# Fronts of two groups side by side: the front's steps move to earlier slots and its self projections to another PSUM bank

## The chip, the cores and the metric
One core of a Trainium2 chip runs the whole program. The metric is device time in microseconds (us) of one execution, the median of several runs. TensorE (PE) does matrix products into the eight banks of PSUM, VectorE (DVE) and ScalarE (ACT) do elementwise work and read PSUM, GpSimd (POOL) does elementwise work in SBUF and issues scattering DMAs, and SyncE (SP) issues the other DMAs. Each engine works through its own queue in order; semaphores couple them.

## The reference
The input is x of 64 batches by 64 tokens by 128 features, a context of the same shape and a mask. Three stages follow one another:

```
h  = layernorm(x)                                   # per token
q, k, v = LN(h Wq), LN(ctx Wk), LN(ctx Wv)          # 16 heads of 8; LN with gamma, beta
q', k' = relu(q) + eps, (relu(k) + eps) * mask;  v = v * mask
att = (q' (k'^T v)) / (q' sum(k') + eps)            # linear attention, per head
x1 = x + LN(att Wd + bd)
z  = layernorm(x1);  h = LN1(z)
x2 = z + softmax(causal(q k^T / sqrt 8)) v Wp + bp  # q, k, v from h: causal self attention
a  = LN2(x2); logits = a Wg + bg; two best of 8 experts, weights by softmax
out = x1 + x2 + sum over the two experts of  w_e (gelu(a W1_e + b1_e) W2_e + b2_e)
```

Mean removal of q, k, v and of the dense output is folded into the weights, so only sums of squares are left of those norms.

## The kernel before
The 4096 tokens are taken as 8 groups of 512 (four tiles of 128 tokens, two batches a tile). Each group passes through a *front* (linear attention up to the self attention's q, k, v), eight *units* of self attention (a tile and half of the heads each), a *back* (output projection, norm, gate logits, two best experts, slots) and a scatter of its rows to DRAM, sorted by expert. When all groups are done, an expert loop of 71 blocks of 128 rows runs, and the results are gathered.

`schedule` (L263) writes the order out by hand, the same for all four compute engines. Each has a function `slot(n, unit, nxt, later, prev, routed)` and a *beat* calls it for n = 0 to 7. In beat k, slot n does unit n of group k, and beside it pieces of the front of group k+1 (`nxt`), of the first norm and the transposes of group k+2 (`later`), of the back of group k-1 (`prev`), and of the routing of group k-2 (`routed`). Ahead of the beats stand `opening(0)`, `front(0)` and `opening(1)` in a line. Beats 2 to 5 are a loop of two turns with two beats each; the others are written out. `finish` does the back of group 7.

A unit on PE: `subtract_max(n)` (waits for the row maxima that DVE took of the scores, `score_max`), `scores(n+1)` (waits for the keys `km`, which POOL multiplies out in `head_keys`), `probs_values(n-1)`, `probs_T(n)`. ACT takes exp in between and copies the transposed probabilities. So PE runs at most one unit ahead of DVE's maxima.

PSUM banks: two for scores, one for transposed probabilities, one for probabilities times values, three front banks F0, F1, F2, and `end_bank` for the transposes of x and context and for the back. Front of group k+1 in beat k before the change, by slot:

- 0: PE `project_k`, `project_q`, `project_v` into F1, F2, F0; ACT `squares`; POOL `x_and_mask`
- 1: DVE `qkv_sums` (one sum over all three); POOL `qkv_scale` (one power)
- 2: DVE `qkv_normal`, `keys_affine`; POOL `values`
- 3: PE `q_T`, `key_sums`, `key_values`; DVE `q_eps`, `key_values`
- 4: PE `linear_attention` in two parts; DVE `divide`
- 5: PE `attention_T`, `dense`; ACT `copy_aT`, `square_o`; DVE `o_sums`; POOL `o_scale`
- 6: DVE `residual` (x1 and its moments); POOL `zh_scale`
- 7: DVE `h_normal`; PE `h_T`, `project_self` into F1, F2, F0; ACT `copy_hT`, `keys`; DVE `unit0_keys`, `queries`; then in slot 0 of the next beat DVE `self_values`, `z_normal`

`later` has `x_moments`, `x_scale` in slot 5 and `x_normal`, `context_T`, `x_T` in 7. `prev` has `y_T` in 0, `project_out` on PE in 1 and on DVE in 3, `a_scale` and `keep_residual` on POOL in 3, `a_normal` in 4, `a_T` in 5, `gate_logits` and `copy_logits` in 6, `top_two` and `gates` in 7. `routed` has `ranks` and `slots` in 2 and two of eight scatters in each of slots 4 to 7.

Of the kernel before, what the change touches and what calls it, by code (L numbers as in the profile page):

```python
# [22 lines left out]
def xattn_attention_moe(nc: bass.Bass, a, out):  # L23
# [28 lines left out]
    with ExitStack() as ctx:  # L52
# [6 lines left out]
        def sems(names):  # L59
# [56 lines left out]
        xa = place[5][:, 2, :, :]  # L116

# [11 lines left out]
        rs = sb("rs", [P, 3 * T])  # L129
        ss = sb("ss", [P, 3 * T])  # L130
        kvz = sb("kvz", [P, T, BPT, HD + 1, 32])
# [67 lines left out]
         kf_ps, qf_ps, vf_ps, km0_ok, km_ok, s_ps, mx_ok, sm_ps, p_ok, pT_ps, pT_ok, y_ok, pv_ps, yT_ps, yT_ok,  # L199
         f_ps, a_ok, aT2_ps, h2T_ok, lg_ps, consts, w_ready, res_ok, mid_ps, y2_ps, sq_ok, o2_ok, dl_ok, e_ok, mid_ok, setup, x_var, x_rstd, x1_ok,  # L200
         ss_ok, qkv_rstd, value_step, oss_ok, o_rstd, z_var, z_rstd, z_ok, zb_ok, a_var, a_rstd, xa_ok, xs_b,
         sum_ok, kn_ok, key_step, den_step, osum_ok, og_ok, zs_b, kb0_ok, rden_ok, as_b, top_ok, topi_ok, gate_step, zeroed, centred,
# [4 lines left out]
            "kv_ps kvz_ok qp_ok au_ps att_ok aT_ps aT_ok o_ps h_ok hT_ps hT_ok kf_ps qf_ps vf_ps km0_ok km_ok "  # L207
# [3 lines left out]
            "z_ok zb_ok a_var a_rstd xa_ok xs_b sum_ok kn_ok key_step den_step osum_ok og_ok zs_b kb0_ok "  # L211
# [51 lines left out]
        def schedule(eng, opening, front, slot, finish):  # L263


            def beat(k, u):
                fixed = isinstance(k, int)
                nxt = None if fixed and k + 1 >= GROUPS else (k + 1, 1 - u)
                later = None if fixed and k + 2 >= GROUPS else (k + 2, u)
                prev = None if fixed and k < 1 else (k - 1, 1 - u)  # L270
                routed = None if fixed and k < 2 else (k - 2, u)
                for n in range(UNITS):
                    slot(n, (k, u), nxt, later, prev, routed)
# [21 lines left out]
        with nc.Block() as block:  # L295
# [79 lines left out]
            def _(pe):  # L375
# [13 lines left out]
                def context_T(k, u):  # L389
                    pe.wait_ge(c_loaded[u], (k // 2 + 1) * 16)  # L390
                    if isinstance(k, int) and k == 1:
                        pe.wait_ge(xT_ok, 1)
                    elif not (isinstance(k, int) and k < 3):
                        pe.wait_ge(lg_ok, k - 2)
# [8 lines left out]
                def project_k(k):  # L403
                    pe.wait_ge(cT_ok, k + 1)
                    if not (isinstance(k, int) and k == 0):
                        pe.wait_ge(kf_ok, k)
                    per_tile(F1, cT, wx[:, 1, :]).then_inc(k_ps, 1)

                def project_q(k):
                    pe.wait_ge(xT_ok, k + 1)  # L410
                    if not (isinstance(k, int) and k == 0):
                        pe.wait_ge(qbd_ok, 2 * k)
                    per_tile(F2, xnT, wx[:, 0, :]).then_inc(q_ps, 1)

                def project_v(k):
                    if not (isinstance(k, int) and k == 0):
                        pe.wait_ge(vbd_ok, k)
# [14 lines left out]
                def key_values(k):  # L432
                    pe.wait_ge(vp_ok, k + 1)
                    pe.wait_ge(qr_ok, k + 1)
                    for b in range(BPT):
                        for t in range(T):
# [3 lines left out]

                def linear_attention(k, part):


# [3 lines left out]
                    for c in range(HD + 1):  # L447
                        dst, at = (front_bank[part], c * S) if c < HD else (F2, part * S)
                        for b4 in range(4):
                            t, b = 2 * part + b4 // 2, b4 % 2  # L450
                            last = pe.matmul(dst[b4 * 32:b4 * 32 + 32, at:at + S], kvz[:, t, b, c, :],  # L451
                                             qp[:, t * P + b * S:t * P + b * S + S], start=True, stop=True)
                    last.then_inc(au_ps, 1)

                def attention_T(k):
                    pe.wait_ge(att_ok, k + 1)
                    for part in range(2):
                        for n4 in range(4):
                            last = pe.transpose((F2, F0)[part][:, n4 * P:n4 * P + P],
                                                att[:, part, n4 * P:n4 * P + P], ident[:, :])  # L460
                    last.then_inc(aT_ps, 1)

                def dense(k):
                    pe.wait_ge(aT_ok, k + 1)
                    pe.matmul(t4(F1[:, :]), ones_r[:, :], over_t(db_hi[:, :]), start=True, stop=True)
                    pe.matmul(t4(F1[:, :]), ones_r[:, :], over_t(db_lo[:, :]), start=False, stop=True,
                              skip_group_check=True)
                    for t in range(T):
                        last = pe.matmul(t4(F1[:, :])[:, t, :], xnT[:, t * P:t * P + P], wx[:, 3, :],
# [7 lines left out]
                def project_self(k):  # L477
                    pe.wait_ge(hT_ok, k + 1)
                    h = h1T[:, :, :].rearrange("p t n -> p (t n)")
                    pe.matmul(F1[:, :], wf[:, 1, :], h, start=True, stop=True).then_inc(kf_ps, 1)  # L480
                    pe.matmul(F2[:, :], wf[:, 0, :], h, start=True, stop=True).then_inc(qf_ps, 1)  # L481
                    per_tile(F0, h, wf[:, 2, :]).then_inc(vf_ps, 1)


                def scores(k, u, n):
                    if n == 0:
                        pe.wait_ge(qbd_ok, 2 * k + 1)
                        pe.wait_ge(km0_ok, k + 1)
                    else:
                        if n == 1:  # L490
                            pe.wait_ge(qbd_ok, 2 * k + 2)
                        pe.wait_ge(km_ok, k * (UNITS - 1) + n)
# [34 lines left out]
                def y_T(k, u):  # L527
                    pe.wait_ge(y_ok, (k + 1) * T)

                    opened = k + 3  # L530
                    pe.wait_ge(xT_ok, min(opened, GROUPS) if isinstance(k, int) else opened)
                    if not (isinstance(k, int) and k == 0):
# [7 lines left out]
                def a_T(k, u):  # L540
                    pe.wait_ge(a_ok, k + 1)
                    transposes(end_bank, send[u][:, :, 0, 0:D]).then_inc(aT2_ps, 1)

                def gate_logits(k):
                    pe.wait_ge(h2T_ok, k + 1)
                    lg = end_bank[:, 0:T * E].rearrange("p (t e) -> p t e", t=T)
# [19 lines left out]
                def opening(k, u):  # L566
                    context_T(k, u)
                    x_T(k)

                def front(k, u):  # L570
# [946 lines left out]
```

## Time and profile before

| | us |
|---|---|
| median of 3 runs | 775.77 (774.07 to 776.71) |
| the profiled execution | 775.02, span 773.2 |
| PE busy | 579.9 (75%) |
| DVE busy | 426.1 (55%) |
| POOL busy | 321.8 (42%) |
| ACT busy | 230.8 (30%) |
| mean granted TensorE clock | 0.822 of full |

Busy time is time in which an engine executes an instruction; the span is from the first instruction to the last. PE work shows longer where the clock was granted at half, so its busy time is no fixed amount of work.

### The profile page before, as it was taken

To read this page: it belongs to the slowest core of one execution; us is meant where nothing else is said; L and a number is where in the kernel's file an instruction comes from. 1 tells how busy PE (TensorE), PEld (TensorE's weight loads), DVE (VectorE), ACT (ScalarE), POOL (GpSimd) and SP (SyncE) were. 2 spreads that over 40 slices of the span, in tenths; PEclk is the share of its full clock that TensorE was granted. 3 is DMA by queue.
4 is the path that set the end of the run, shared out by engine and by line. 5 is a ranking of instruction groups with operands and counts; after the bars stand their busy time and mean duration, and the time that the engine had idled before them with its cause. 6 is when DMAs were issued, how large, how long until landed. Compare 5 with 4: busy or idle time off the path is not lost.

```text
span 773.2 us, 15557 instructions
## 1 busy us (share of the span) xinstructions
PE 579.9 (75%) x4384; PEld 461.9 (60%) x4385; DVE 426.1 (55%) x1285; ACT 230.8 (30%) x559; POOL 321.8 (42%) x327
## 2 busy tenths in 40 slices
PE   0463897988877978978879778795249999998960
PEld 0362576666655657656566566564148887787860
DVE  4424456686767676576685774673513433333435
ACT  0101313414313403313322331331024444444430
POOL 5302341451464563463562562463714334334340
PEclk9755758887979878879787898797559999999995
DMA  5996260250430250170000000000135555555639
GB/s 131 176 205 108 62 78 2 68 71 1 92 54 15 77 76 8 31 120 14 14 0 7 22 0 9 14 8 28 41 106 158 149 158 153 157 158 147 166 95 322
DMA packets 90461, 63.85 MB, mean 83 GB/s; under 512 B 16302, under 2 KB 77105, under 8 KB 90420
## 3 DMA queue, kind: packets, MB, share of 16 engines
q1 hardware_dynamic: 86100, 54.86, 33.0%
q0 software_dynamic: 4320, 8.47, 3.1%
q8 instruction: 22, 0.36, 0.2%
q14 instruction: 19, 0.16, 0.1%
HBM read 35.18 MB, written 28.58 MB: 82 GB/s over the span
## 4 chain that ended last, share of the span: by engine, by line
PE 55%; DVE 15%; issue 11%; ACT 4%; SPq 4%; POOL 4%; DMA 3%; DVEq 1%; another core or an unknown queue 1%; ACTq 0%; POOLq 0%
PE bank L678 9%; PE bank L667 7%; PE bank L497 6%; PE bank L522 5%; PE bank L380 4%; PE bank L451 4%; PE bank L437 3%; PE bank L385 2%; PE bank L480 2%; DVE places L1102 2%; PE bank L509 2%; PE bank L429 2%; PE bank L481 2%; POOL sorted_rows L983 2%; PE bank L502 2%
## 5 line engine op out<-in xcount | busy, mean ns | idle before, releaser
L1046 POOL DMA_INDIRECT result_rows<-back,rows x71 | 69.4, 978 | 117.6 <-DVE back L1466 109.8
L845 ACT ACTIVATE mid<-bank,b 128x128 f32<-128x128 f32 x284 | 81.2, 369 | 92.3 <-PE bank L667 80.5
L522 PEld LDWEIGHTS bank<-vbd,pT 128*128 128x128 f32 x512 | 74.6, 216 | 44.4 <-issue 24.2
L963 POOL TENSOR_TENSOR km<-kb,head 128x512 f32<-128x512 f32 x56 | 59.5, 1069 | 80.2 <-ACT kb L752 49.1
L678 PE MATMUL bank<-w,mid 128*128 x568 | 83.8, 292 | 11.0 <-ACT mid L845 9.2
L678 PEld LDWEIGHTS bank<-w,mid 128*128 128x128 f32 x568 | 71.2, 194 | 24.2 <-issue 23.0
L667 PE MATMUL bank<-hT,w 128*128 128x128 f32 x568 | 83.0, 291 | 3.1 <-DMA w<-in_L_ffn_exp_W_dram 1.6
L522 PE MATMUL bank<-vbd,pT 128*128 128x36 f32 x512 | 74.2, 295 | 13.9 <-ACT pT L765 13.1
L914 POOL TENSOR_TENSOR rs<-ve,minus_half 128x12 f32<-128x12 f32 (+2 forms) x24 | 39.8, 1660 | 97.4 <-DVE ve L1149 48.5
L667 PEld LDWEIGHTS bank<-hT,w 128*128 128x128 f32 x568 | 71.1, 197 | 5.9 <-issue 4.4
L497 PE MATMUL bank<-km,qbd 128*128 128x512 f32 x128 | 73.3, 658 | 0.0
L765 ACT COPY pT<-bank 128x512 f32<-128x512 f32 x64 | 37.8, 590 | 117.7 <-PE bank L509 110.3
L1213 DVE TENSOR_REDUCE mx<-bank 128x8 fp32r<-128x512 f32 x64 | 44.1, 689 | 48.4 <-PE bank L497 48.0
L983 POOL DMA_INDIRECT sorted_rows<-send,slot_u x64 | 63.4, 990 | 16.7 <-issue 16.7
L385 PE MATMUL bank<-ident,places 128*128 128x128 f32 x160 | 33.8, 352 | 45.3 <-DVE places L1069 23.1
L759 ACT ACTIVATE pr<-bank 128x512 f32<-128x512 f32 x64 | 38.6, 602 | 93.0 <-PE bank L502 85.5
L1461 DVE TENSOR_TENSOR plain<-bank,b 128x128 f32<-128x128 f32 x71 | 20.7, 291 | 66.2 <-PE bank L678 35.9
L1455 DVE TENSOR_SCALAR hT<-bank,cols 128x128 f32<-128x128 f32 x71 | 29.1, 410 | 50.0 <-PE bank L659 49.5
L385 PEld LDWEIGHTS bank<-ident,places 128*128 128x128 f32 x160 | 25.3, 190 | 51.7 <-DVE places L1069 25.8
L509 PE MATMUL bank<-ident,pr 128*128 128x128 f32 x256 | 42.1, 289 | 0.2 <-issue 0.2
L502 PE MATMUL bank<-mx,neg_ident 128*128 128x512 f32 x64 | 32.6, 509 | 6.6 <-DVE mx L1213 6.5
L429 PE MATMUL bank<-emb,places 128*128 128x2 f32 x64 | 14.6, 350 | 27.1 <-DVE places L1111 27.1
(187 smaller groups left out, 1004.1 us busy)
## 6 DMA issues: line engine op xcount, KB each, us to landing
w<-in_L_ffn_exp_W_dram SPq DMA_DIRECT2D x79, 256.0 KB, 3.4
sorted_rows<-blank SPq DMA_DIRECT2D x64, 260.0 KB, 7.6
rows<-sorted_rows SPq DMA_DIRECT2D x71, 65.0 KB
places<-result_rows SPq DMA_DIRECT2D x16, 256.0 KB, 5.5
places<-in_ctx_dram SPq DMA_DIRECT2D x8, 256.0 KB, 2.9
places<-in_x_dram SPq DMA_DIRECT2D x8, 256.0 KB, 3.8
out_dram<-acc SPq DMA_DIRECT2D x8, 256.0 KB, 5.9
result_rows<-back,rows POOLq DMA_INDIRECT x71
```

What stands on the lines that cost most here:

```text
L385: last = pe.transpose(t4(psum[:, :])[:, t, :], src[:, t, :], ident[:, :])
L497: pe.matmul(bank_n[:, :], qbd[u][:, n % 2, n // 2, :], km[n % 2][:, :, :], start=False, stop=True).then_inc(s_ps, 1)
L502: pe.matmul(score_bank[n % 2][:, :], neg_ident[:, :], mx[:, n % 2, :].unsqueeze(2).broadcast_to([P, HG, S]), start=False, stop=True, skip_ ...
L509: last = pe.transpose(probT_bank[:, j * P:j * P + P], pr[:, n % 2, j * P:j * P + P], ident[:, :])
L522: last = pe.matmul(pv_bank[:, hp * W:hp * W + W].rearrange("p (b c) -> p b c", b=BPT), pT[:, j, :], vbd[u][:, t, :, hp, :], start=True, st ...
L667: last = pe.matmul(hidden[2 * (s % 2) + c // 2][:, c % 2 * P:c % 2 * P + P], w1[s % 4][:, c * P:c * P + P], hT[s % 2][:, :], start=True, s ...
L678: last = pe.matmul(result[s % 2][:, 0:D], mid[s % 2][:, c, :], w2[:, bass.ds(expert, 1), c, :].rearrange("p o d -> p (o d)"), start=c == 0 ...
L845: A(mid[s][:, c, :], hidden[2 * s + c // 2][:, c % 2 * P:c % 2 * P + P], ACT.Gelu, bias=b1[:, bass.ds(expert, 1), c]).then_inc(mid_ok, 1)
L963: G.tensor_tensor(km[n % 2][:, :, :], kb[u][:, n % 2, t * S:t * S + S].unsqueeze(1).broadcast_to([P, HG, S]), head8[:, :].unsqueeze(2).bro ...
L983: G.indirect_dma_start(out=sorted_dram, out_offset=bass.IndirectOffsetOnAxis(ap=slot_u[u][:, j // 2, t:t + 1], axis=0), in_=send[u][:, t, ...
L1046: G.indirect_dma_start(out=result_dram, out_offset=bass.IndirectOffsetOnAxis(ap=rows[s][:, D:D + 1].bitcast(U32), axis=0), in_=back[s % 4] ...
L1213: V.tensor_reduce(mx[:, n % 2, :], score_bank[n % 2][:, :].rearrange("p (h k) -> p h k", h=HG), AX.X, ALU.max).then_inc(mx_ok, 1)
```

## The change
What it does, part by part:

- `schedule` has no `opening` and `front` any more. The beats start at k = -2: beats -2 and -1 have no unit, only pieces of the groups 0 and 1.
- The front of a group is spread over two beats. As `later` (group k+2): `x_moments` in slot 1, `x_normal` in 2, `context_T` and `x_T` in 3, `project_k` and `project_q` in 5, `project_v` and the sums in 6, `qkv_normal` and `values` in 7. As `nxt` (group k+1): `q_T`, `key_sums`, `key_values` in 0, `linear_attention` and `divide` in 1, `attention_T`, `dense`, `o_sums` in 2, `residual`, `o_scale`, `zh_scale` in 3, `h_normal` and `h_T` in 4, self keys and queries, `z_normal` in 5, self values in 6.
- `project_self` is split: keys and values go to `end_bank`, one after the other, queries to F0. The waits on the banks follow (`gate_logits`, `a_T`, `y_T`, `context_T`, `project_k`, `project_v`).
- `prev`: DVE's `project_out` and POOL's `a_scale`, `keep_residual` in slot 2, `a_normal` in 3, `a_T` in 4, `gate_logits` and `copy_logits` in 7. `routed`: `ranks` and `slots` in 4, scatters 2, 2 and 4 in slots 5, 6 and 7.
- Squares, sums and powers are done for each of k, q, v by itself. Keys are scaled by their norm and gamma in one instruction per tile; values are scaled by norm times mask, and beta times mask is a new tile `vb`, so POOL's `values` has two steps for three. The attended transpose has a tile `aT` of its own, the norms of the dense output and of x1 have small tiles of their own.
- The denominators of the linear attention are computed first and signalled by themselves (`den_ps`); `divide`, `attention_T` and `copy_aT` go by halves.
- `unit0_keys` leaves DVE: POOL's `head_keys` does all eight, two slots ahead of their unit.

The core of the diff (declarations, and edits that say the same again, are left out):

```diff
-            opening(0, 0)
-            front(0, 0)
-            opening(1, 1)
-            beat(0, 0)
-            beat(1, 1)
+            for k in range(-2, 2):
+                beat(k, k % 2)
...
 PE, slot
                     if prev:
                         if n == 0:
                             y_T(*prev)
                         if n == 1:
                             project_out(prev[0])
-                        if n == 6:
+                        if n == 4:
+                            a_T(*prev)
+                        if n == 7:
                             gate_logits(prev[0])
                     if nxt:
+                        if n == 0:
+                            q_T(nxt[0])
+                        if n == 1:
+                            linear_attention(nxt[0], 0)
+                        if n == 2:
+                            attention_T(nxt[0])
+                        if n == 6:
+                            self_values(nxt[0])
+                    if later:
+                        if n == 3:
+                            context_T(*later)
+                        if n == 5:
+                            project_k(later[0])
+                            project_q(later[0])
+                    if unit:
+                        probs_T(k, n)
+                    if nxt:
                         if n == 0:
                             key_sums(nxt[0])
                             key_values(nxt[0])
+                        if n == 1:
+                            linear_attention(nxt[0], 1)
+                        if n == 2:
+                            dense(nxt[0])
+                        if n == 4:
+                            h_T(nxt[0])
+                        if n == 5:
+                            self_keys(nxt[0])
+                            self_queries(nxt[0])
+                    if later:
+                        if n == 3:
+                            x_T(later[0])
+                        if n == 6:
+                            project_v(later[0])
...
 DVE, slot (new order; score_max(n+1), slots in 4 and attended stand first)
+                    if nxt:
+                        if n == 0:
+                            q_eps(nxt[0])
+                            key_values(nxt[0])
+                        if n == 1:
+                            divide(nxt[0])
+                        if n == 2:
+                            o_sums(nxt[0])
+                        if n == 3:
+                            residual(*nxt)
+                        if n == 4:
+                            h_normal(*nxt)
+                        if n == 5:
+                            z_normal(*nxt)
+                            queries(*nxt)
+                    if later:
+                        if n == 1:
+                            x_moments(*later)
+                        if n == 2:
+                            x_normal(*later)
+                        if n == 5:
+                            mask_columns(*later)
+                        if n == 6:
+                            sums(later[0], 0)
+                            sums(later[0], 1)
+                    if prev:
+                        if n == 2:
+                            project_out(*prev)
+                        if n == 3:
+                            a_normal(*prev)
+                    if nxt and n == 6:
+                        self_values(*nxt)
+                    if later:
+                        if n == 6:
+                            sums(later[0], 2)
+                        if n == 7:
+                            qkv_normal(later[0])
...
 POOL, slot
+                    if unit and n + 2 < UNITS:
+                        head_keys(*unit, n + 2)
+                    if unit and n == 0:
+                        z_bias(*unit)
+                    if prev and n == 2:
                         a_scale(prev[0])
                         keep_residual(*prev)
+                    if nxt:
+                        if n == 3:
+                            o_scale(nxt[0])
+                            zh_scale(nxt[0])
+                        if n == 6:
+                            head_keys(*nxt, 0)
+                        if n == 7:
+                            head_keys(*nxt, 1)
+                    if routed and n == 5:
+                        scatter_waits(*routed)
+                    if later:
+                        if n == 1:
+                            x_scale(later[0])
+                        if n == 5:
+                            x_and_mask(*later)
+                        if n == 6:
+                            qkv_scale(later[0])
+                        if n == 7:
+                            values(later[0])
+                    if routed and n >= 5:
+                        for j in ((0,), (1,), (2, 3))[n - 5]:
+                            scatter(*routed, j)
```

## Rows read from the trace of the kernel before

**Rows 1.** The page: busy time of PE, and the granted clock in 40 slices.
```profile
PE 579.9 (75%) x4384; PEld 461.9 (60%) x4385; DVE 426.1 (55%) x1285; ACT 230.8 (30%) x559; POOL 321.8 (42%) x327
PEclk9755758887979878879787898797559999999995
```
**Rows 2.** Windows cut at beats' first exps: length, busy by engine, PE clock, DMA share, GB/s.
```profile
83.69:142.30 58.61, 51.65 (x367) 39.20 (x367) 34.29 (x84) 16.44 (x30) 20.35 (x17) 0.73 0.30 47
...
258.21:319.91 61.70, 51.53 (x398) 39.45 (x398) 41.41 (x129) 18.32 (x34) 30.58 (x27) 0.81 0.27 53
...
443.11:503.80 60.69, 48.77 (x390) 36.49 (x390) 39.08 (x116) 17.23 (x32) 30.12 (x28) 0.83 0.03 10
503.80:526.83 23.03, 21.96 (x139) 16.06 (x138) 16.20 (x59) 9.37 (x18) 14.38 (x14) 1.00 0.05 16
...
526.83:566.90 40.07, 10.59 (x56) 8.84 (x55) 14.58 (x74) 3.37 (x8) 20.62 (x21) 0.56 0.10 33
```
**Rows 3.** Chain that ended last, beat from 258.21: start, us, what.
```profile
274.59 1.64 DVE places L1109
276.26 1.16 DVE places L1111
277.46 1.87 PE bank L429 x8
279.33 3.02 PE bank L437 x16
```
**Rows 4.** Windows of two beats with the granted clock, columns as in rows 2.
```profile
256.00:276.00 20.00, 15.78 (x104) 11.54 (x102) 14.96 (x32) 7.16 (x13) 13.01 (x12) 1.00 0.63 121
276.00:286.00 10.00, 8.54 (x34) 6.88 (x34) 7.11 (x18) 0.60 (x1) 6.36 (x6) 0.50 0.27 38
288.00:303.00 15.00, 12.92 (x168) 9.89 (x162) 8.31 (x27) 4.77 (x9) 4.52 (x5) 1.00 0.05 16
...
250.00:254.00 4.00, 3.49 (x4) 1.52 (x5) 0.56 (x4) 1.79 (x4) 0.00 (x0) 0.50 0.05 17
```
**Rows 5.** Timeline, PE: start, us, line, out<-in, count, idle before.
```profile
250.51 2.08 PE L480 MATMUL bank<-h1T,wf 128*128 128x512 f32 x2 [0.87 <-ACT h1T L746]
...
259.54 1.95 PE L380 MATMUL bank<-wx,places 128*128 128x128 f32 x16
...
262.58 0.46 PE L502 MATMUL bank<-mx,neg_ident 128*128 128x512 f32 x1
...
266.11 0.46 PE L502 MATMUL bank<-mx,neg_ident 128*128 128x512 f32 x1
...
277.46 1.87 PE L429 MATMUL bank<-emb,places 128*128 128x2 f32 x8 [4.08 <-DVE places L1111]
...
290.25 1.21 PE L451 MATMUL bank<-places,kvz 128*32 128x64 f32 x72
```
**Rows 6.** Groups of the beat 258.21 to 319.91, DVE: count, busy us, mean ns, idle before.
```profile
L1201 DVE TENSOR_TENSOR vbd<-bank,bv_b 64x256 f32<-64x256 f32 x5 | 2.1, 423 | 0.1
L1191 DVE TENSOR_SCALAR qbd<-bank,cols 64x256 f32<-64x256 f32 x4 | 1.9, 483 | 0.1
L1125 DVE TENSOR_TENSOR kvz<-bank,head 128x512 f32<-128x512 f32 x2 | 1.9, 1029 | 1.7 <-PE bank L437 1.7
...
L1109 DVE TENSOR_TENSOR places<-places,beta_b 128x512 f32<-128x512 f32 x1 | 1.6, 1633 | 0.0
...
L1184 DVE TENSOR_TENSOR km<-kb,head 128x512 f32<-128x512 f32 x1 | 0.7, 691 | 4.0 <-ACT kb L752 4.0
```
**Rows 7.** The same beat, POOL.
```profile
L983 POOL DMA_INDIRECT sorted_rows<-send,slot_u x8 | 8.0, 997 | 1.9 <-issue 1.9
L963 POOL TENSOR_TENSOR km<-kb,head 128x512 f32<-128x512 f32 x7 | 7.4, 1069 | 9.0 <-ACT kb L752 6.3 <-PE bank L497 2.7
...
L974 POOL TENSOR_TENSOR acc<-x,places 128x512 f32 x1 | 1.3, 1268 | 0.0
L914 POOL TENSOR_TENSOR e_rs<-e_ve,minus_half 128x4 f32<-128x4 f32 x1 | 1.1, 1122 | 0.9 <-DVE e_ve L1240 0.9
```
**Rows 8.** Window of DVE's residual step in that beat, columns as in rows 2.
```profile
302.39:305.88 3.49, 2.96 (x16) 2.67 (x14) 3.31 (x16) 1.60 (x3) 0.96 (x1) 0.63 0.12 38
```

More of the change, by code:

```diff
@@ L116, in xattn_attention_moe @@
         xa = place[5][:, 2, :, :]
+        aT = place[5][:, 3, :, :].rearrange("p t d -> p (t d)")
         em = lanes("em", [P, T])
@@ L261, in xattn_attention_moe, with schedule @@
         ]
-        def schedule(eng, opening, front, slot, finish):
+        def schedule(eng, slot, finish):
             def beat(k, u):
                 fixed = isinstance(k, int)
-                nxt = None if fixed and k + 1 >= GROUPS else (k + 1, 1 - u)
+                unit = None if fixed and k < 0 else (k, u)
+                nxt = None if fixed and not 0 <= k + 1 < GROUPS else (k + 1, 1 - u)
                 later = None if fixed and k + 2 >= GROUPS else (k + 2, u)
@@ L439, in key_values, with attend @@
                     last.then_inc(kv_ps, 1)
+                def attend(dst, k, part, c):
+                    for b4 in range(4):
+                        t, b = 2 * part + b4 // 2, b4 % 2
+                        last = pe.matmul(dst[b4 * 32:b4 * 32 + 32, :], kvz[:, t, b, c, :],
+                                         qp[:, t * P + b * S:t * P + b * S + S], start=True, stop=True)
+                    return last
                 def linear_attention(k, part):
@@ L446, in linear_attention @@
                         pe.wait_ge(qp_ok, k + 1)
[L447 to L452, printed above, removed]
+                        for f in range(2):
+                            last = attend(F2[:, f * S:f * S + S], k, f, HD)
+                        last.then_inc(den_ps, 1)
+                    for c in range(HD):
+                        last = attend(front_bank[part][:, c * S:c * S + S], k, part, c)
                     last.then_inc(au_ps, 1)
                 def attention_T(k):
-                    pe.wait_ge(att_ok, k + 1)
                     for part in range(2):
+                        pe.wait_ge(att_ok, 2 * k + 1 + part)
                         for n4 in range(4):
@@ L649, in _ @@
                 pe.wait_ge(w_ready, 1)
-                schedule(pe, opening, front, slot, finish)
+                schedule(pe, slot, finish)
                 turned, hidden, result = bank[0:2], (bank[2], bank[4], bank[5], bank[6]), (bank[3], bank[7])
@@ L833, in _ @@
                 act.wait_ge(w_ready, 1)
-                schedule(act, opening, front, slot, finish)
+                schedule(act, slot, finish)
                 hidden = (bank[2], bank[4], bank[5], bank[6])
@@ L1040, in finish @@
                         scatter(k, u, j)
-                schedule(pool, opening, front, slot, finish)
+                schedule(pool, slot, finish)
                 def send_back(i, s):
@@ L1300, in slots @@
                     V.tensor_copy(seen_bf[:, :], seen[:, :]).then_inc(seen_ok, 1)
-                def opening(k, u):
-                    x_moments(k, u)
-                    x_normal(k, u)
-                def front(k, u):
-                    mask_columns(k, u)
-                    qkv_sums(k)
-                    qkv_normal(k)
-                    keys_affine(k)
-                    q_eps(k)
-                    key_values(k)
-                    divide(k)
-                    o_sums(k)
-                    residual(k, u)
-                    h_normal(k, u)
-                    unit0_keys(k, u)
-                    queries(k, u)
@@ L1361, in slot @@
                         top_two(prev[0])
-                    if nxt and n == 7:
-                        h_normal(*nxt)
-                    if n == UNITS - 1:
+                    if unit and n == UNITS - 1:
                         attended(k, u, n)
```

398 lines of the change are left out of this document (153 added, 245 removed).

## The prediction
> **What bounds the kernel now.** I read the page, then a table of windows cut where each beat's first exp starts, then the chain of waits of one beat, then PE, DVE and POOL rows of that beat. On the page no engine is full and TensorE's clock sits below full until the expert stage [rows 1]. The window rows cut the span: 83.7 us until beat 0's first exp; seven beats with a front in them, 420.1 us together (503.80 less 83.69), 55.7 to 62.2 each; a last beat without a front, 23.0 us; 40.1 us until the expert loop; then the expert loop, which the change doesn't touch [rows 2]. A beat of 61.7 us has PE busy for 51.5 and DVE for 41.4, while the beat without a front needs 23 us for the same eight units at full clock. So the 38 us that a front adds are the subject: PE's own work in them, latency of its chain, and lost clock.
>
> The chain of waits shows the latency: in slot 3 DVE finishes keys (its addition ends at 276.2, one more operation at 277.4) and only then PE runs key_sums at 277.46 and key_values at 279.33 [rows 3], 1.87 and 3.02 us, both at half speed. The clock rows say why half: PE sat idle 4.1 us before 277.46 [rows 5], and the granted clock reads 1.00 from 256 to 276, 0.50 from 276 to 286, 1.00 again from 288 [rows 4]: the two levels, 2.4 and 1.2 GHz. The stretch at 250 to 254 is the second kind, after the gap before the self projections [rows 4, 5]. There are fourteen such stretches in the seven beats, two a beat, 7 to 17 us long and mostly near 10. After work resumed the full clock was back 9.4 us later in one (277.5 to 286.9) and 5.2 in another (250.5 to 255.7).
>
> **The change, slot by slot.** Work removed: DVE's unit-0 keys (0.69, [rows 6]), now an eighth head_keys on POOL (1.07, [rows 7]); q, v and k normalisation goes from 6.0 us on DVE (three at 0.68, then 1.27, 1.63 [rows 6], 1.15) to 3.7 (four short ones 1.13, 0.69, 0.16, 0.65, 0.45, 0.65). Added: three pairs of sums for one, 2.6 against 1.9. DVE falls from 41.4 to 39.1 us busy. POOL gains two small powers (about 1.2) and a key multiply, and stays near 32 busy. PE's work is the same matmuls, and ACT's copies and squares only move with them (18.3 of 61.7 us busy, [rows 2]). The sum therefore isn't about work but about order, and I walk one steady beat on full-clock durations. One unit on PE costs 2.66 (the two subtractions at 262.58 and 266.11 are 3.53 apart with an 0.87 project_out between [rows 5]); 16 projections hold PE for 1.79 (1.95 with their drain, [rows 5]) and 8 for 0.88; key_sums 0.9 and key_values 1.5 (half of rows 3); each half of linear_attention 1.2 [rows 5]; each self projection 0.9 to 0.95 (half of 2.07, [rows 5]). Time 0 is subtract_max(0).
>
> Slot 0: PE runs the unit, y_T, q_T, key_sums and key_values until 5.25; DVE's multiply into kvz (2 x 1.03, [rows 6]) waits for it and ends at 7.3. Slot 1: PE 5.1 to 11.15; divide's second half follows at 11.95, x_moments to 13.45. Slot 2: dense ends at 16.0, ACT squares, o_sums runs 16.8 to 17.7; x_normal 1.1; project_out 2.25: 21.05. Slot 3 has the new wait. residual needs o_scale, which on POOL's queue now stands behind a_scale (1.12), keep_residual (1.27) and head_keys(5) (1.07) [rows 7], and a_scale waits for the end of project_out. So o_scale ends at 25.5 and DVE, having only score_max(4) to do, idles 3.8 us. Behind head_keys(5) PE's scores(5) waits too, until 24.6. Residual takes 3.5 [rows 8], a_normal 1.1: 30.2. PE's a_T waits for that, idle 27.0 to 30.3. Slot 4: score_max(5) 0.7, slots 1.75, attended 0.9, h_normal 1.1: 34.7; PE's h_T waits, idle 31.2 to 34.8. Slot 5: in front of the self keys stand the unit and now the next group's 16 projections, so the self queries end only at 41.4; DVE's queries (4 x 0.48, [rows 6]) at 43.5. From there DVE is the bound without a break: slot 6 costs 6.05 (max 0.72, attended 0.9, sums 2.7, self_values 4 x 0.42 [rows 6]), slot 7 with the next score_max(0) 8.3 (normalising 4.0 and a 0.35 wait, logits 0.2, top two 1.2, attended 0.9, gates 0.95, max 0.7). Next beat's subtraction: 58.2. PE has nothing from 53.2 to 58.0, since it may run only one unit ahead of DVE's maxima.
>
> The same walk on the beat of before, with its half-clock stretches taken at full speed, gives about 53 (61.7 less 6.3 in slots 3 and 4 and 2.4 in the self projections). So at equal clock the new order is 5 us longer: PE's idle sums to 19 us against 10 in the beat of before, and DVE's 15 lie in places where nothing else is queued that could run.
>
> **The clock.** Both long gaps (3.3 and 3.6 us back to back before slot 5; 4.8 before slot 0) are near the 4.1 us gap that was followed by a half stretch. Each lies ahead of PE work that sets the end: 5.1 us in slot 0, 6.6 in slots 4 and 5. If the full clock returns 5.2 us after work resumes, each costs 2.6; if 9.4 us after, 4.7. Middle 3.65 each, 7.3 a beat: 65.5. I bound the beat by 58.2 (no stretch) and 67.6 (two long ones).
>
> **First and last beats.** Beat 0 has no previous group, so no project_out, a_normal, gates or wait at o_scale, and no slots: 11.3 less. Beat 1 lacks slots: 1.8 less. Beat 6 has no later group (x_moments 1.5, x_normal 1.1, sums 2.7, normalising 4.0, projections): 10 less. Together 7 x 65.5 - 23.1 = 435.4 against 420.1: +15.3. Ahead of beat 0 the sums per projection and the shorter key and value steps bring key_values from 43.0 to 38.0, the separate den result and split divide bring the dense output from 58.1 to 48.4, h_normal from 67.1 to 56.7; then group 1's projections and normalisation (about 3.6 on PE at half clock, 6.7 on DVE) stand in the line, and the first exp comes at 76.9 for 83.7: -7. Bounds -11 and 0. Beat 7 starts after a gap and runs its first units at half clock: +3 (0 to 4). Behind it, slots and eight scatters of group 6 start earlier, but the last scatter still waits for group 7's slots, which a_scale, placed behind four scatters at 1.3 each, delays by 1.6; 0 in sum, against the 40.1 us of [rows 2] (bounds -2 and +3). SP issues group k+2's loads and fills once group k's transposes and xpb are done: now in slot 5 of beat k-2, in the kernel before in slot 1 of beat k-1; their first use is slot 1 of beat k, over a beat later, so they stay hidden (uncovered they would cost their 3 to 4 us of landing).
>
> Sum: 775.0 for the profiled execution (span 773.2 and 1.8 around it) + 15.3 - 7 + 3 = 786.3. The median of the runs shown lies 0.7 above the profiled one: 787.
>
> A row that a rule bears on: DVE's key addition with both inputs in SBUF took 1.63 [rows 6] while POOL added values beside it, and a key multiply of the same shape took 0.69 with POOL idle [rows 6]. The walk uses 0.69 and 0.45 in slot 7 since POOL there does powers and scatters. The Trainium skill, "SBUF — State Buffer", section "SBUF: two separate sides", calls the pair of ports that the two engines share an exclusive lock for the whole instruction, also for operations with two SBUF inputs; by it the powers, which read SBUF too, could hold those operations up. By the trace's own rows that would be at most 0.94 and 0.7 more, 1.6 a beat and 11 us in all; it is inside the high end of the range.
>
> **Rivals.**
> A, as above, two half-clock stretches a beat: 63.4 to 67.6 a beat, so 772 to 802. Chance 0.50.
> B, the clock holds through at least one of the gaps: one stretch, 61.9 a beat, gives 761, none gives 384.3 - 420.1 - 7, which is 732. For it: PE's work lies denser than before in slots 0 to 2 and 5 to 6; against it: the 4.1 us gap was followed by a stretch, and no beat of before has fewer than two. The point from which it decides is 64 us a beat: 7B - 23.1 - 4 = 420.1. Chance 0.22.
> C, the overlap does what slots' plain loads allow, since POOL's and DVE's queues run further ahead than in my walk: the sum of each slot's longer engine is about 48, with 3 of latency 51 a beat, near 682. Against: o_sums, residual and h_T each need a result of the same slot. Chance 0.04.
> D, worse than A: port contention 1.6 a beat, and the four scatters in slot 7 (5.3 us) let head_keys(2) come late into slot 1, where I count only 0.3 us of slack: 70 a beat, 818. Chance 0.14.
> E, beats stay as long as they are (60 on average), because what the front gained is lost in the same tail; only the opening gains: 768. Chance 0.10.
>
> **How the numbers follow.** Changes below 0.3% (2.3 us) can't be told from none. Faster: nearly all of B, C and E and a sliver of A: 0.38. Same: the lower part of A: 0.08. Slower: 0.54. Likeliest 787, its own range 772 to 802. For 8 in 10 I take in B with one stretch and most of D: 755 to 812; below are C and B without stretches, above the rest of D.
>
> **What would show it.** A beat of 63 to 68 between first exps. POOL's o_scale power waiting until project_out's end plus some 3.5 us, and DVE idle before the residual. PE idle 3 us or more before a_T, before h_T and before subtract_max(0), with granted clock 0.50 behind the second and third. First exp near 77. Wrong would be: beats under 62 or a clock near 1.00 through slots 5 and 0 (B), PE busy over 85% of a beat (C), or a first exp later than 84.

## The result, and the profile after

The changed kernel took 798.59 us (median of 4 runs, 794.42 to 803.61) beside 775.05 us for the kernel before (774.07 to 776.71): 1.030 times, 95% interval 1.024 to 1.037. Slower, as forecast (787), and inside the range. In two later batches it took 797.19 and 798.16 us; the kernel before took between 751.96 and 775.05 us over five batches, so the sign is safe and the size is 3 to 6%.

The page of the changed kernel, its busy line and granted clock (answers to [rows 1]):
```profile
PE 563.2 (71%) x4384; PEld 449.3 (57%) x4385; DVE 436.4 (55%) x1333; ACT 235.7 (30%) x559; POOL 333.6 (42%) x359
PEclk9768798956968878696696886686559999999995
```
Windows cut where each beat's first exp starts: the opening, beats 0, 4 and 6, the beat without a front, and the stretch until the expert loop (answers to [rows 2], same columns):
```profile
0.00:72.69 72.69, 29.82 (x275) 24.68 (x277) 44.08 (x121) 12.37 (x21) 31.30 (x63) 0.81 1.02 172
72.69:129.83 57.14, 44.41 (x367) 33.30 (x367) 33.43 (x90) 16.94 (x30) 22.47 (x23) 0.83 0.49 80
329.21:393.39 64.18, 47.63 (x398) 36.07 (x398) 43.22 (x134) 18.97 (x34) 28.17 (x29) 0.79 0.02 5
458.06:517.18 59.12, 48.36 (x366) 34.88 (x366) 32.04 (x105) 16.20 (x29) 25.98 (x26) 0.73 0.04 13
517.18:545.42 28.24, 24.60 (x129) 17.74 (x128) 13.88 (x38) 9.47 (x18) 13.72 (x14) 0.84 0.04 12
545.42:585.00 39.58, 12.63 (x66) 10.76 (x65) 16.12 (x88) 3.46 (x8) 20.63 (x21) 0.52 0.10 33
```
The difference of the two spans (792.7 - 773.2 = 19.5) splits by these cuts: opening -11.0 (72.7 for 83.7), the seven beats +24.4 (444.5 for 420.1), the last beat +5.2 (28.2 for 23.0), all behind it +0.9. Between first exps the seven beats are 57.1, 66.1, 64.3, 69.0, 64.2, 64.7 and 59.1 us. PE is busy for less of a beat than before (47.6 us of 64.2 in beat 4, against 51.5 of 61.7 in the beat that the prediction walked), and DVE for slightly more (43.2 against 41.4, where 39.1 was forecast): the beat got longer by idle time of PE and DVE.

Where it idles, from the timeline of beat 4 (start us, us, engine, line, operation, idle before and what ended it):
```profile
328.38 0.80 PE L518 MATMUL bank<-mx,neg_ident 128*128 128x512 f32 x1 [7.49 <-DVE mx L1200]
...
351.31 1.01 POOL L915 TENSOR_TENSOR e_rs<-e_ve,minus_half 128x4 f32<-128x4 f32 x1 [5.97 <-DVE e_ve L1227]
352.29 1.26 POOL L976 TENSOR_TENSOR acc<-x,places 128x512 f32 x1
353.51 1.04 POOL L965 TENSOR_TENSOR km<-kb,head 128x512 f32<-128x512 f32 x1
354.51 1.02 POOL L915 TENSOR_TENSOR o_rs<-o_ve,minus_half 128x4 f32<-128x4 f32 x1
354.61 0.39 PE L511 MATMUL bank<-causal,ident_bf 128*128 128x512 bf16 x1 [2.15 <-POOL km L965]
355.56 1.13 DVE L1150 SCALAR_TENSOR_TENSOR x<-bank,o_rs,gamma_b 128x128 f32<-128x128 f32 x4 [3.64 <-POOL o_rs L915]
358.96 1.11 DVE L1058 TENSOR_SCALAR send<-places,e_mv,e_rs 128x128 f32<-128x128 f32 x4
360.13 1.12 PE L391 MATMUL bank<-ident,send 128*128 128x128 f32 x4 [2.40 <-DVE send L1058]
361.12 1.05 DVE L1282 TENSOR_TENSOR seen<-seen,added 128x8 f32<-128x8 f32 x1
362.34 0.84 DVE L1286 CAST slot_u<-slot_f 128x8 uint32<-128x8 f32 x1
363.72 1.04 POOL L927 TENSOR_TENSOR vb<-em,beta_b 128x512 f32<-128x512 f32 x1
364.07 2.50 DVE L1058 TENSOR_SCALAR places<-x,x_mv,z_rs 128x128 f32<-128x128 f32 x4
364.72 1.26 POOL L931 TENSOR_TENSOR places<-places,beta_b 128x512 f32<-128x512 f32 x1
366.63 1.12 PE L391 MATMUL bank<-ident,places 128*128 128x128 f32 x4 [4.53 <-DVE places L1058]
374.82 1.99 DVE L1178 TENSOR_SCALAR qbd<-bank,cols 64x256 f32<-64x256 f32 x4 [3.12 <-PE bank L498]
387.06 1.05 POOL L965 TENSOR_TENSOR km<-kb,head 128x512 f32<-128x512 f32 x1
387.18 2.17 DVE L1246 TENSOR_TENSOR dlt<-top 128x4 f32<-128x4 f32 x1
388.06 1.26 POOL L941 TENSOR_TENSOR places<-places,gamma_b 128x512 f32<-128x512 f32 x1
392.56 0.80 PE L518 MATMUL bank<-mx,neg_ident 128*128 128x512 f32 x1 [3.04 <-DVE mx L1200]
```
DVE's residual (L1150) waits 3.64 us for o_scale (`o_rs`), which POOL runs after `a_scale` (`e_rs`), `keep_residual` (`acc`) and the key multiply (`km`), the queue order that the walk named. The gaps of PE are 2.4 before a_T, 4.5 before h_T and 3.0 before subtract_max(0), which is the last row. Not in the walk: h_normal (the second L1058 of DVE) took 2.50 us where a_normal, the first, took 1.11. Three operations on a few elements took 1.05 (`seen`), 0.84 (`slot_u`) and 2.17 (`dlt`), where each takes 0.17 further on in the same trace, behind the beats. POOL had 128x512 operations under way beside all four.

The granted clock around the two later gaps (windows, columns as above):
```profile
355.90:366.60 10.70, 3.80 (x19) 3.25 (x16) 10.34 (x35) 1.36 (x2) 6.93 (x8) 0.50 0.00 1
366.60:369.80 3.20, 3.17 (x9) 2.03 (x10) 0.00 (x0) 1.26 (x2) 1.61 (x2) 0.56 0.12 42
369.80:375.00 5.20, 5.20 (x35) 4.03 (x34) 1.90 (x6) 2.67 (x6) 0.00 (x0) 1.00 0.00 0
...
392.60:396.60 4.00, 4.00 (x11) 2.47 (x12) 0.69 (x1) 0.79 (x2) 3.36 (x4) 0.50 0.15 50
396.60:402.00 5.40, 5.40 (x47) 4.62 (x47) 3.94 (x5) 2.24 (x4) 2.30 (x3) 0.99 0.00 2
```
Two half-clock stretches a beat, at the places forecast, but once PE had work again the full clock was back after 3.2 and 4.0 us, not 5.2 to 9.4. Most of each stretch fell into time in which PE had little to do; the part under work cost about 1.6 and 2.0 us, half its length.

### The profile page after: what moved, and what is told of

Same layout as the page of the kernel before. It is cut to its first block, busy times and chain, and to the rows that moved or that the text cites. A ratio compares the mean times of both kernels' runs of the same rounds, so it can differ in the third digit from the quotient of the medians.

```text
span 792.7 us, 15673 instructions
## 1 busy us (share of the span) xinstructions
PE 563.2 (71%) x4384; PEld 449.3 (57%) x4385; DVE 436.4 (55%) x1333; ACT 235.7 (30%) x559; POOL 333.6 (42%) x359
## 4 chain that ended last, share of the span: by engine, by line
PE 39%; issue 22%; DVE 17%; POOL 13%; ACT 3%; SPq 2%; DMA 2%; ACTq 0%; DVEq 0%; POOLq 0%
PE bank L685 9%; PE bank L674 7%; PE bank L513 4%; POOL sorted_rows L985 4%; POOL km L965 3%; PE bank L386 3%; PE bank L538 3%; DVE places L1058 3%; PE bank L391 2%; ACT mid L846 2%; PE bank L525 2%; PE bank L450 1%; PE bank L518 1%; DVE ss L1085 1%; SPq L305 1%
## 5 line engine op out<-in xcount | busy, mean ns | idle before, releaser
L538 PEld LDWEIGHTS bank<-vbd,pT 128*128 128x128 f32 x512 | 79.7, 227 | 34.8 <-issue 23.7
L965 POOL TENSOR_TENSOR km<-kb,head 128x512 f32<-128x512 f32 x64 | 66.5, 1043 | 72.3 <-ACT kb L758 54.3
L513 PE MATMUL bank<-km,qbd 128*128 128x512 f32 x128 | 85.9, 761 | 0.0
L538 PE MATMUL bank<-vbd,pT 128*128 128x36 f32 x512 | 77.2, 303 | 7.1 <-ACT pT L771 6.6
L985 POOL DMA_INDIRECT sorted_rows<-send,slot_u x64 | 65.7, 1027 | 32.4 <-issue 32.4
L674 PEld LDWEIGHTS bank<-hT,w 128*128 128x128 f32 x568 | 70.3, 195 | 4.7 <-issue 3.3
L518 PE MATMUL bank<-mx,neg_ident 128*128 128x512 f32 x64 | 37.8, 590 | 36.3 <-DVE mx L1200 35.7
L525 PE MATMUL bank<-ident,pr 128*128 128x128 f32 x256 | 47.7, 318 | 0.1
L511 PE MATMUL bank<-causal,ident_bf 128*128 128x512 bf16 x64 | 30.9, 484 | 18.8 <-POOL km L965 15.6
L518 PEld LDWEIGHTS bank<-mx,neg_ident 128*128 128x128 f32 x64 | 14.3, 224 | 52.5 <-DVE mx L1200 49.1
```

Source lines behind the costliest of these rows:

```text
L513: pe.matmul(bank_n[:, :], qbd[u][:, n % 2, n // 2, :], km[n % 2][:, :, :], start=False, stop=True).then_inc(s_ps, 1)
L518: pe.matmul(score_bank[n % 2][:, :], neg_ident[:, :], mx[:, n % 2, :].unsqueeze(2).broadcast_to([P, HG, S]), start=False, stop=True, skip_ ...
L525: last = pe.transpose(probT_bank[:, j * P:j * P + P], pr[:, n % 2, j * P:j * P + P], ident[:, :])
L538: last = pe.matmul(pv_bank[:, hp * W:hp * W + W].rearrange("p (b c) -> p b c", b=BPT), pT[:, j, :], vbd[u][:, t, :, hp, :], start=True, st ...
L674: last = pe.matmul(hidden[2 * (s % 2) + c // 2][:, c % 2 * P:c % 2 * P + P], w1[s % 4][:, c * P:c * P + P], hT[s % 2][:, :], start=True, s ...
L965: G.tensor_tensor(km[n % 2][:, :, :], kb[u][:, n % 2, t * S:t * S + S].unsqueeze(1).broadcast_to([P, HG, S]), head8[:, :].unsqueeze(2).bro ...
```

## The experiments

The beats at the loop's ends differ from the others, so beside each median stands the mean of beats 1, 2, 4 and 5 ("steady beat"): 64.8, 65.0 and 65.2 us in three profiles of the changed kernel, 59.8 and 58.6 in two of the kernel before. A steady beat comes from one profiled run, which lay up to 8 us from the median of its kernel (789.05 for 797.19 us), and a single beat differs by 1 to 3 us from its neighbours. All were edits of the changed kernel but one.

**o_scale ahead of keep_residual and a_scale.** POOL, slot 2 and 3:
```
 if nxt and n == 2:  o_scale(nxt[0])
 if prev and n == 2: keep_residual(*prev); a_scale(prev[0])     # order swapped
 if nxt and n == 3:  zh_scale(nxt[0])                           # o_scale gone from here
```


> POOL's slot 2 and 3 in another order: o_scale ahead of keep_residual and a_scale, keep_residual ahead of a_scale. Theory 1 (the order of the queues sets the beat): DVE's wait before the residual, 3.6 us a beat in six beats, goes; beats near 61 for 64.6, 777 us. Theory 2 (the lost TensorE clock sets it): the gaps ahead of slots 5 and 0 stay, so no more than 1 us a beat, 792. Theory 3 (VectorE and GpSimd holding each other up): no change but where keep_residual lands beside a VectorE operation.

Measured: 769.54 us (767.49 to 770.92) in a batch where the kernel before took 756.58, ratio 1.0185 (1.011 to 1.026). The changed kernel itself did not run in that batch; in its three others it lay at 797 to 799. The steady beat is 62.0. DVE's residual group in the changed kernel, then in this one (busy, mean ns, idle before):
```profile
L1150 DVE SCALAR_TENSOR_TENSOR x<-bank,o_rs,gamma_b 128x128 f32<-128x128 f32 x32 | 9.0, 344 | 22.2 <-POOL o_rs L915 22.0
```
```profile
L1151 DVE SCALAR_TENSOR_TENSOR x<-bank,o_rs,gamma_b 128x128 f32<-128x128 f32 x32 | 8.9, 343 | 0.1
```
The wait is gone and about 3 us a beat with it: this wait was on the path. A part came back elsewhere: DVE's wait for the bank of the self queries rose from 29.2 to 33.9 us over eight beats.

**Scatters 0 and 1 ahead of the values' two products** (POOL slot 5: `scatter_waits`, em, `scatter 0`, `scatter 1`, then vb and xpb):

> In POOL's slot 5 the two scatters stand ahead of vb and xpb, so that these run after h_normal. Theory 3: h_normal takes 1.1 us for 2.5 and the beat is 1.4 us shorter, 789 us. Theory 1: h_normal's length is as before, 798. If issuing a scatter holds VectorE up as well, h_normal stays near 2.5.

Measured: 788.26 us (784.28 to 791.59), ratio to before 1.042 (1.034 to 1.050). That median is 9 to 10 us under the changed kernel's in its three batches and near the 789 of theory 3, but the changed kernel did not run beside it. The steady beat is 64.8, not shorter, read from the slowest of the four runs (791.59). So whether the beat gained is not settled. h_normal of beat 5 in the timeline, and the clock from h_T on in windows:
```profile
429.38 1.16 DVE L1063 TENSOR_SCALAR places<-x,x_mv,z_rs 128x128 f32<-128x128 f32 x4
429.44 1.06 POOL L989 DMA_INDIRECT sorted_rows<-send,slot_u  x1 [0.49 <-issue]
```
```profile
430.50:434.50 4.00, 3.92 (x11) 2.50 (x11) 0.21 (x2) 1.26 (x2) 3.23 (x4) 0.50 0.10 33
434.50:438.00 3.50, 3.50 (x29) 3.26 (x29) 1.54 (x5) 1.29 (x3) 0.00 (x0) 0.96 0.00 0
```
h_normal is short (1.16 for 2.50) while a scatter is issued beside it, so it was POOL's elementwise operations that held DVE back. The Trainium skill ("SBUF — State Buffer", section "SBUF: two separate sides") states that the pair of ports which VectorE and GpSimd share is locked for a whole instruction, on VectorE's side by operations with two SBUF inputs and by those in a two-port mode. The rows agree for `dlt` and `seen`, which have two such inputs; `slot_u` and h_normal have one, and no run shows their mode. Part of the gain was lost behind it: h_T starts 1.3 us sooner behind a_T and then runs at half clock for 4.0 us and not 3.2.

**The next group's sums from slot 6 to slot 5** (DVE takes them while it would wait for the self queries):
```
 if later and n == 5: sums(later[0], 0); sums(later[0], 1)      # were in n == 6
```


> DVE's first two sums stand in slot 5 between z_normal and queries, where it waits 3.1 us for the self queries, for slot 6. Theory 1 (DVE is bound from queries to the next score_max(0)): the tail is 1.7 us shorter in six beats, 788 us. Theory 2: PE is what is late, no change, 798.

Measured: 784.78 us (782.04 to 788.82), ratio 1.038 (1.031 to 1.046); steady beat 64.0, again from the slowest of four runs. DVE's wait for the queries' bank fell by 20.6 us over eight beats, from 29.2 to 8.6. About 1 us a beat came of it in the profile, and the median lies 12 to 14 us under the changed kernel's in other batches: some of that wait was idle time that the later slots made up.

**The second head's key mask to slot 6, the values ahead of scatters 1 to 3 in slot 7**, meant to leave no elementwise operation of POOL beside the router's small ones:

> The changed kernel with the second head's key mask moved from slot 7 to slot 6 and the values' two products ahead of the scatters 1 to 3 in slot 7, so that the POOL operations beside the router's small DVE operations are DMA issues. Theory (POOL's tensor operations hold back DVE's small operations there): dlt falls from 2.17 to 0.17 us and its beat by up to 2.0 us in six beats, 8 to 12 us in all, ratio to the changed kernel 0.985 to 0.99, ratio to before 1.015 to 1.02. Rival (dlt is off the path, since the scores' maximum follows it with slack): ratio to the changed kernel 1.00 within 0.003 though dlt is short. Second rival (the contention only moves to another small operation): dlt short, another 128x4 or 128x8 operation of DVE over 1 us, ratio 1.00.

> The changed kernel once more, as the measure for e8_values_first on the same chip: 1.028 to 1.035 times the kernel before, beats 2 to 5 of 64 to 68 us, the router's difference (dlt, 128x4) 2.17 us a beat beside two 128x512 operations of POOL.

Measured on one chip: 796.01 us (791.94 to 797.34) for 798.16 us (795.45 to 803.41), 0.997 times; the two ratios to before, 1.056 (1.050 to 1.061) and 1.060 (1.054 to 1.066), overlap. The group in the changed kernel, then in this one:
```profile
L1246 DVE TENSOR_TENSOR dlt<-top 128x4 f32<-128x4 f32 x8 | 9.4, 1169 | 0.3
```
```profile
L1245 DVE TENSOR_TENSOR dlt<-top 128x4 f32<-128x4 f32 x8 | 1.3, 166 | 0.3
```
The delay is gone and the time is not: the theory fell. (`dlt` did not come to stand beside DMA issues as meant. In beat 4 it starts at 390.50, just when POOL's first product of the values has ended and the second begins.) The mask that moved stands in slot 6 and the residual's wait is still there. The steady beat went from 65.2 to 64.4, within the spread of single beats, and the beat at the loop's jump (below) from 70.3 to 72.5. A blocked operation seen in the trace is not yet a cost.

**Unread matmuls in PE's gaps.** 37 a beat, a 128x128 identity product into banks nobody reads:
```
 fill(10, F2)              # ahead of a_T
 fill(15, F2)              # ahead of h_T
 fill(12, score_bank[1])   # ahead of subtract_max(0)
```


> 37 matmuls a beat that nobody reads stand where PE waits: 10 before a_T, 15 before h_T, 12 before subtract_max(0), 0.22 us each at full clock. Theory 1: the waits stay, only the work after them runs at full clock; half clock costs 1.6 us behind h_T and 2.0 behind subtract_max(0) in the changed kernel's trace, so up to 3.6 a beat, 773 us, less what the fill overshoots. Theory 2: the clock is the whole loss and more, beats of 58 and under, 752 us or less. If the fill is late for the gaps, the time rises.

Measured: 766.81 us (763.13 to 772.25), ratio 1.018 (1.009 to 1.027); mean clock 0.868 for 0.811; steady beat 61.3, 3.5 under the first profile. The residual's wait stayed at 22.0 us. So the fill gave back about 3.5 us a beat, close to the 1.6 and 2.0 read above, and this is separate from the order's price. It is not the whole price of the clock: in the steady beats the granted clock went up from 0.76 or 0.79 to between 0.86 and 0.89, not to 1.00.

**The four order edits together, and with unread matmuls** (2 ahead of a_T, 16 ahead of h_T, 12 ahead of subtract_max(0)), beside the changed kernel and the kernel before with 24 unread matmuls a beat:

> The changed kernel, not edited, on this chip, so that the others have it as their reference. All theories: 1.03 to 1.05 of the kernel before.

> Changed kernel with four moves together: o_scale and keep_residual ahead of a_scale; scatters ahead of vb and xpb in slot 5; two of DVE's sums in slot 5; POOL's head_keys(1) in slot 6 and its values ahead of the scatters in slot 7. Theory 1 with 3: 3.3 + 0.6 + 0.9 from the single runs and 1.1 for DVE's small subtraction that no longer waits for POOL's multiply, 6 us a beat, 40 us off the changed kernel, near 0.99 of the kernel before. Theory 2: what is saved in waits comes back as half clock, 20 us off at most, near 1.015.

> The four moves, and 30 matmuls a beat that nobody reads in PE's gaps (2 before a_T, 16 before h_T, 12 before subtract_max(0)). Theory 1: 3 us a beat below the four moves alone, 0.96 of the kernel before. Theory 2: more than that, 0.94. If the gaps have become too short for the fill: no better than the four moves.

> The kernel before with matmuls that nobody reads in its gaps: 15 before key_sums, 6 before x_T and 3 before the self projections. By my walk the half-clock stretches cost 8.7 us of its beats, so if the fill holds the clock 5 to 8 us a beat go, ratio 0.93 to 0.95. If half clock costs the beat of before no more than it did the changed one (3.1 a beat in e4), 0.97. If the gaps carry the loss and not the clock: 1.00.

| one batch, before 773.87 us | us | ratio to before | clock | steady beat |
|---|---|---|---|---|
| changed | 797.19 | 1.032 (1.028 to 1.035) | 0.814 | 65.0 |
| four order edits | 761.18 | 0.982 (0.980 to 0.985) | 0.825 | 58.7 |
| four edits + unread matmuls | 731.50 | 0.943 (0.937 to 0.949) | 0.884 | 55.0 |
| before + unread matmuls | 750.39 | 0.969 (0.965 to 0.974) | 0.887 | 58.2 |

The four edits took 36 us off the changed kernel, where theory 1 said 40. Beat 4 of the four edits without and with the unread matmuls, each the shortest steady beat of its profile:
```profile
313.08:369.75 56.67, 45.52 (x398) 34.03 (x398) 40.26 (x134) 18.89 (x35) 25.70 (x25) 0.86 0.01 4
```
```profile
288.23:342.04 53.81, 49.02 (x460) 39.35 (x460) 40.84 (x134) 18.87 (x35) 26.97 (x27) 0.97 0.02 6
```
With its POOL and DVE orders mended the overlap beats the kernel before by 1.8% in this batch. It ran in no other, and in three batches the kernel before took 752 to 759 us, less than these 761; so that the order edits alone win is not safe. With the unread matmuls it wins by 5.7%. Held against a kernel before that gets the same kind of filling it is 2.5% faster (731.5 for 750.4).

The filled kernel before also tests the prediction's other walk, which put its beat of 61.7 us at 53 with the clock full. Two of its beats ran at a granted clock of 1.00, beats 1 and 3, and took 52.9 and 55.1 us (55.7 and 61.7 in the first profile of before). The beats with a clock of 0.89 to 0.94 took 55.1 to 60.8, so its steady beat of 58.2 is not one with the clock held.

**Two kernels once more, in another batch.**

> The kernel before, unedited, with a profile of its own. It took 773.87 us in one batch and 751.96 us in another, while the changed kernel took 797.19 and 798.16 us. Theory: the 22 us lie in the half-clock stretches of its seven beats, which fall otherwise there; then a profile of about 750 us shows beats of 53 to 60 us with fewer stretches below 0.6 of the clock and a mean clock of 0.83 or more, and the opening and the expert loop as they were. Rival: they lie in the loads of the opening (first exponential at 65 us in place of 83.7) or in the expert loop (206 us).

> The same kernel as e7_four_fill, beside the kernel before in another batch. If its gain is its own it takes 724 to 735 us again whatever the kernel before takes: a ratio of 0.94 to 0.95 where that takes 774 us and of 0.965 to 0.975 where it takes 752 us. If the 731.5 us were luck of its half-clock stretches it lies above 740 us.

Measured: the kernel before 756.97 us (755.53 to 759.83), the filled one 726.06 (724.65 to 727.68), ratio 0.956 (0.954 to 0.959) to the 759.02 us of the batch's other runs of before. Its gain is its own. Of the 19.1 us by which this profile of before is shorter than the first (754.1 for 773.2), 9.7 lie in the seven beats, 2.7 in the opening and 6.7 behind beat 7's first exp: neither theory holds alone, and the mean clock is the same (0.823 for 0.822). Why the kernel before differs by 3% between batches while the changed one stays within 1.5 us stays open.

## Why the prediction was right, and where it was off

**Right.** The order of the walk, step by step: o_scale behind three POOL operations (3.64 us measured for 3.8), PE's gaps at three places, two half-clock stretches, more idle and not more work. Removing that wait alone gave 3 us a beat. Rival A is what happened: its steady beat was to be 63.4 to 67.6, and was 64.8. That it came so near the 65.5 is luck, since two of the terms were wrong. The part behind the beats moved by 0.9 where 0 was said.

**Mis-sized, in opposite directions.** The clock was put at 7.3 a beat, from 5.2 and 9.4 us until the full clock returned; it measured 3.2 and 4.0, 3.6 us a beat. Port contention was put at 0, and at most 1.6; beat 4 shows 4.9 us of it (1.4 in h_normal, 2.0 in `dlt`, 1.5 in the routing's `seen` and `slot_u`), and DVE was busy for 43.2 us where 39.1 was forecast. The prediction named the two additions of slot 7 as those at risk and said that POOL does powers and scatters there. Beside the powers they took 0.69 and 0.44, as the walk had them. But the change itself also puts a key multiply and the two products of `values` into POOL's slot 7, and `dlt` met those; the others were met in slot 4. So the contention of rival D came, with 4.9 us of delay for its 1.6 and about 3 of it on the path, but without its beat of 70 us.

Where the time went shows when the walk is laid beside beat 4 (us from the start of subtract_max(0), at 328.38):

| end of | walk | beat 4 | late by |
|---|---|---|---|
| o_scale | 25.5 | 27.2 | 1.7 |
| a_normal | 30.2 | 31.7 | 1.5 |
| h_normal | 34.7 | 38.2 | 3.5 |
| queries | 43.5 | 48.4 | 4.9 |
| the beat (next subtract_max(0)) | 58.2 | 64.2 | 6.0 |

Until a_normal (1.5) and between h_normal and the queries (1.4) stand the half-clock stretches under work, about 3 together. Between a_normal and h_normal (2.0) and behind the queries (1.1) stand the held-up operations, again about 3. So 58.2 (walk), 3 to 3.6 (clock) and about 3 (contention) make the measured 64.2 to 64.8. This is read from places; no run took all of the contention away. The four order edits took 6.3 us off a steady beat (65.0 to 58.7), of which o_scale's wait is 3; in single profiles the other three gave 0.2, 1.0 and 0.8. The two errors cancel, so beats 2, 4 and 5 came out 0.8 to 1.3 under the forecast's 65.5; its error in the seven beats lies in the others: beat 0 +2.9, beat 1 +2.4, beat 3 +3.5, beat 6 +3.6. What beats 0 and 6 lack was taken off whole, while part of it may have been beside other work; no run separates that, and beat 0 was 57.1, 51.2 and 56.3 us in the three profiles.

The walk's own 58.2 without a half stretch can be compared: without the 3.6 us of the o_scale wait it is 54.6, and the kernels with four edits and unread matmuls have steady beats of 55.0 and 55.9 at a granted clock of 0.85 to 0.97. It is a loose comparison, since the edits also took off part of the queries' wait and some contention and half clock were left.

**Missed: the end of the loop's turn.** Beat 3 ends the loop's first turn and is 69.0 us, 4.2 over the steady beat. The maxima of the next turn's first unit, in the changed kernel, in the one with four edits, and in that with the unread matmuls:
```profile
327.63 0.69 DVE L1200 TENSOR_REDUCE mx<-bank 128x8 fp32r<-128x512 f32 x1 [4.28 <-issue]
```
```profile
311.50 0.69 DVE L1205 TENSOR_REDUCE mx<-bank 128x8 fp32r<-128x512 f32 x1 [7.43 <-issue]
```
```profile
286.96 0.69 DVE L1212 TENSOR_REDUCE mx<-bank 128x8 fp32r<-128x512 f32 x1 [6.95 <-issue]
```
It is the first operation behind the jump back to the loop's start, and DVE waited for nothing that the profile shows; at the other beats' ends it starts at once or within 0.5 us. With 37 unread matmuls a beat the gap is on PE, at its own first operation behind the jump:
```profile
303.85 0.60 PE L511 MATMUL bank<-causal,ident_bf 128*128 128x512 bf16 x1 [6.07 <-issue]
```
In the kernel before, DVE passes the same place almost without a gap:
```profile
315.45 0.69 DVE L1184 TENSOR_TENSOR km<-kb,head 128x512 f32<-128x512 f32 x1 [3.97 <-ACT kb L752]
...
318.65 0.69 DVE L1213 TENSOR_REDUCE mx<-bank 128x8 fp32r<-128x512 f32 x1 [0.48 <-PE bank L497]
```
There it waits 3.97 us for ACT's keys a little ahead of the jump (3.43 at the end of beat 1, where no jump is). The change took that operation from DVE. So a jump does not cost 4 us by itself; whether the wait ahead of it hid the cost in the kernel before, or something else of the new order makes it, stays open, and no run unrolled the loop. It bears on the single edits too: beat 3 was 66.1 to 72.5 us with them, 4 to 8 over their steady beats against 3 to 5 in the changed kernel's three profiles, so part of what a steady beat gained was lost there.

**Smaller terms.** The opening ended at 72.7 (76.9 forecast, 83.7 before). The second group's projections and normalisation may have found more gaps than the walk gave them; no run separates this. The last beat cost +5.2 for +3. Over all, against the forecast's terms (-7 for the opening): beats +9.1, opening -4.0, last beat +2.2, rest +0.9. That is the 8 us between the profiled run's 794.42 and the 786.3 forecast for it. The other 3.5 of the 11.6 us by which the median missed 787 come from the runs: the median lay 4.2 over the profiled run, not 0.7. One slip in the rivals changes nothing: the 51 us a beat of C give 685 by the prediction's own terms, not 682.

## What to carry to other kernels

Read off, for every step that is moved, what stands ahead of it on each queue that it uses: one power of 1 us placed behind three other operations cost 3 us a beat. Mend the order before judging an overlap, and where a gap of PE ends in work that sets the end, price filling it with unread matmuls. A slow instruction in the trace counts only if taking its delay away shortens the whole: the largest of them here, 2 us a beat, changed the time by 0.3% when it alone was taken away.

## What the hardware showed that was not expected

- An operation on 128x4 elements took 2.17 us where it starts beside the first of two 128x512 elementwise operations of POOL in a row. It ended with the second (at 389.35 and 389.32), so it was held up through both. In the kernel before it took 0.17. Four operations on 128x128 took 1.16 us beside a scatter that POOL issued, and 2.50 beside its products.
- DVE stood 3.2 to 7.5 us without a visible cause at its first operation behind the loop's jump in ten of the eleven profiles of the changed order (in the other PE did, for 6.1), and 0.5 us in the kernel before.
- 30 unread matmuls a beat raised PE's busy time by 18.6 us over the span and shortened the kernel by 30.
